# Turning the token rows of a GNN/attention/MoE layer: the attention branch added by TensorE in PSUM instead of by VectorE and GpSimd

## What is computed

```python
xn = _layernorm(x, axis=-1)
x = x + _L0_gnn_ref(xn, edge_index, edge_attr, ...) + _L0_mix_ref(xn[None], ...)[0]
x = x + _L0_ffn_ref(_layernorm(x, axis=-1)[None], ...)[0]

# end of _L0_gnn_ref
h = relu(h @ W1 + b1) @ W2 + b2
h = (h - h.mean(0)) * rsqrt(h.var(0) + eps) * gamma + beta
return relu(h)                          # y, the MLP's result
# end of _L0_mix_ref
return einsum('bnc,oc->bno', attn, Wproj) + bproj      # the attention rows
# start of _L0_ffn_ref: logits = xt @ Wr + br, top 2 of 8 experts for each node
```

## Time and profile before

| | us |
|---|---|
| time, median of 3 runs | 1186.91 (1179.77 to 1190.77) |
| span of the profiled execution | 1050.8 |
| median less span | 136.1 |
| TensorE matmuls busy | 964.7 (92%) |
| VectorE busy | 671.7 (64%) |
| GpSimd busy | 555.1 (53%) |
| ScalarE busy | 513.5 (49%) |

### The profile page before, as it was taken

How to read it: one execution, slowest core, us unless ns; L and a number is a source line. 1 busy time by engine, 2 the same in 40 slices (tenths; PEclk the granted TensorE clock), 3 DMA queues, 4 the chain that set the end, 5 groups by cost and what they waited for, 6 DMA issues and landing times.

```text
span 1050.8 us, 17977 instructions
## 1 busy us (share of the span) xinstructions
PE 964.7 (92%) x5112; PEld 810.3 (77%) x5113; DVE 671.7 (64%) x1274; ACT 513.5 (49%) x1036; POOL 555.1 (53%) x627
## 2 busy tenths in 40 slices
PE   5898999999999999999998961799999999999994
PEld 4677888888888888877775860778888888888884
DVE  5455565656655565578886778666666666666663
ACT  3644555555454545455554566444444444444442
POOL 3277777777777777777760040224253353444442
PEclk8899999999999999999998986899999999999998
DMA  9667788788888878998762028412545636635321
GB/s 246 197 154 237 255 267 253 250 268 266 260 254 262 269 247 267 278 313 270 239 202 86 26 89 316 181 26 40 204 90 174 220 50 213 192 73 160 98 38 21
DMA packets 85472, 198.30 MB, mean 189 GB/s; under 512 B 19785, under 2 KB 37139, under 8 KB 84378
## 3 DMA queue, kind: packets, MB, share of 16 engines
q1 hardware_dynamic: 55926, 131.60, 36.1%
q0 software_dynamic: 28752, 64.45, 25.5%
q10 hardware_dynamic: 724, 1.42, 0.5%
HBM read 147.86 MB, written 49.97 MB: 188 GB/s over the span
## 4 chain that ended last, share of the span: by engine, by line
POOL 29%; PE 29%; DMA 19%; issue 13%; DVE 7%; ACT 2%; POOLq 1%; SPq 0%; DVEq 0%; ACTq 0%
POOL work L758 29%; DMA out<-work,rowc 11%; PE banks L1141 6%; PE banks L1166 4%; DMA work<-token_table,tokc 4%; PE banks L470 3%; PE banks L446 3%; PE banks L1168 2%; PE banks L969 2%; PE banks L1054 2%; PE banks L1151 2%; DMA work<-in_edge_attr 1%; PE banks L1042 1%; DMA wts<-in_src 1%; DVE st L1776 1%
## 5 line engine op out<-in xcount | busy, mean ns | idle before, releaser
L758 POOL DMA_INDIRECT work<-node_table,srcT x391 | 379.5, 971 | 157.0 <-issue 117.6
L470 PE MATMUL banks<-work 128*128 128x256 f32 x780 | 179.1, 379 | 1.1 <-issue 1.1
L446 PE MATMUL banks<-w_edge,eaT 128*128 128x256 f32 x780 | 179.3, 380 | 0.0
L470 PEld LDWEIGHTS banks<-work 128*128 128x128 f32 x780 | 148.0, 190 | 21.8 <-issue 1.8
L446 PEld LDWEIGHTS banks<-w_edge,eaT 128*128 128x128 f32 x780 | 143.4, 191 | 16.8
L1166 PE MATMUL banks<-wsplit,hidT_hi 128*128 x416 | 153.3, 408 | 2.1 <-DVE hidT_lo L1908 2.1
L529 DVE TENSOR_TENSOR work<-banks,work 128x512 f32<-128x512 f32 x195 | 126.8, 682 | 26.1 <-DMA work<-node_table,srcT 15.2
L1141 PE MATMUL banks<-wsplit,xeT_hi 128*128 x416 | 134.3, 404 | 2.8 <-DVE xeT_lo L1915 2.8
L483 ACT COPY wts<-banks 128x256 f32<-128x256 f32 x66 | 24.6, 372 | 228.8 <-PE banks L470 227.8
L811 POOL DMA_INDIRECT out<-work,rowc x52 | 83.4, 1605 | 82.2 <-ACT work L1441 45.6
L1168 PE MATMUL banks<-wsplit,hidT_lo 128*128 x416 | 116.8, 281 | 0.0
(11 more groups left out here) (263 smaller groups left out, 1555.2 us busy)
## 6 DMA issues: line engine op xcount, KB each, us to landing
wsplit<-split_table SPq DMA_DIRECT2D x8, 4096.0 KB, 15.3
work<-in_edge_attr SPq DMA_DIRECT2D x65, 384.0 KB, 4.6
wts<-in_L_ffn_W SPq DMA_DIRECT2D x64, 256.0 KB, 4.9
split_table<-raw_hi SPq DMA_DIRECT2D x64, 256.0 KB, 3.0
split_table<-raw_lo SPq DMA_DIRECT2D x64, 256.0 KB, 4.3
work<-node_table,srcT POOLq DMA_INDIRECT x391, 4.2
xs<-in_x SPq DMA_DIRECT2D x8, 560.0 KB
wts<-in_L_ffn_b SPq DMA_DIRECT2D x8, 512.0 KB, 4.0
```

The lines of the kernel that those rows point to most:

```text
L446: last = nc.tensor.matmul(b[:, k * DIM:(k + 1) * DIM], eaT[:, u, 2 * q + k], w_edge[:], start=True, stop=True)
L470: last = nc.tensor.matmul(bank[5][:, 0:DIM], onehot[:, u, j], msg[:, u, j], start=(j == 0), stop=(j == GT - 1))
L758: pool.indirect_dma_start(out=xg[n % NB][0:rows, j], out_offset=None, in_=node_table, in_offset=bass.IndirectOffsetOnAxis(ap=srcT[0:rows, ...
```

## The change

The additions on VectorE and GpSimd are gone. TensorE multiplies the attention columns (`qT`) and then the relu's columns (`y_cur`) by the same `turn_route` into the same PSUM region: `attn_turn(q)` starts the sum and `y_turn(q)` ends it. ScalarE's relu now reads and writes in node order, and the step of five moves to the stationary operand of `y_turn`. `attn_turn` of the turns 2, 0, 1 and 3 stands ahead of the relu; the others stand one turn ahead of their `y_turn`, each behind the wait for its banks. SP's wait ahead of the first weight load is now for the last turn on TensorE.

```diff
@@ sync
-            sp.wait_ge(y_first, 1)
-            sp.wait_ge(y_sum, CHUNKS - 1)
+            sp.wait_ge(y_T, 3 * CHUNKS)
             load_weights(sp, 0)
@@ gpsimd
-            for c in range(1, CHUNKS):
-                pool.wait_ge(y_relu, 2 * c + 2)
-                nc.gpsimd.tensor_tensor(y_cur[c], y_cur[c], qT[:, :, c * CHUNK_TILES * TILE:(c + 1) * CHUNK_TILES * TILE],
-                                        ALU.add).then_inc(y_sum, 1)
@@ tensor
-            def y_turn(q):
-                c, b = q // 3, q % 3
-                if q == 0:
-                    pe.wait_ge(y_first, 1)
-                elif b == 0:
-                    pe.wait_ge(y_sum, c)
+            def turn(q, rows, first):
+                for m in range(2 if q % 3 < 2 else 1):
+                    k = 2 * (q % 3) + m
+                    for h in range(HALVES):
+                        last = nc.tensor.matmul(bank[2 * (q % 4) + m][0:TILE, h * P:h * P + P + EXPERTS], rows(h, k),
+                                                turn_route[:, h * (P + EXPERTS):(h + 1) * (P + EXPERTS)],
+                                                start=(first and h == 0), stop=(not first and h == 1), skip_group_check=True)
+                return last
+
+            def attn_turn(q):
+                if q == 1:
+                    pe.wait_ge(z2_ready, 2 * COL_CHUNKS)
                 if q == 3:
                     pe.wait_ge(xw_scaled, 2)
                 if q >= 4:
                     pe.wait_ge(lg_added, q - 3)
-                for m in range(2 if b < 2 else 1):
...
-                last.then_inc(y_T, 1)
-
+                lo = q // 3 * CHUNK_TILES
+                turn(q, lambda h, k: qT[:, h, (lo + k) * TILE:(lo + k + 1) * TILE], True)
+
+            def y_turn(q):
+                c = q // 3
+                pe.wait_ge(y_relu, 2 * c + 2)
+                turn(q, lambda h, k: y_cur[c][:, h, k:CHUNK_TILES * TILE:CHUNK_TILES], False).then_inc(y_T, 1)
+
+            pe.wait_ge(ao_ready, 2 * COL_CHUNKS)
+            for q in (2, 0, 1, 3):
+                attn_turn(q)
             for q in range(3 * CHUNKS):
+                if q >= 4:
+                    attn_turn(q)
                 y_turn(q)
@@ scalar
-                    nc.scalar.activation(y_cur[c][:, o].rearrange("q (k p) -> q k p", k=CHUNK_TILES), by_fives(hT, c)[:, o],
+                    nc.scalar.activation(y_cur[c][:, o], hT[:, o, c * CHUNK_TILES * TILE:(c + 1) * CHUNK_TILES * TILE],
                                          ACT.Relu, bias=bns[:, 3, o:o + 1], scale=bns[:, 2, o:o + 1]).then_inc(y_relu, 1)
@@ vector
-            dve.wait_ge(y_relu, 2)
-            nc.vector.tensor_tensor(y_cur[0], y_cur[0], qT[:, :, 0:CHUNK_TILES * TILE], ALU.add).then_inc(y_first, 1)
```

More of the change, by code:

```diff
@@ L344, in build @@
         y_relu = sem("y_relu")
-        y_sum = sem("y_sum")
-        y_first = sem("y_first")
         y_T = sem("y_T")
```

## The result

| | kernel before | changed kernel |
|---|---|---|
| time, median of 12 runs each | 1181.95 us (1166.25 to 1190.77) | 1187.62 us (1178.53 to 1198.39) |
| changed / before | | 1.0077, 95% interval 1.0041 to 1.0114 |
| span of the profiled execution | 1050.8 us | 1188.1 us |
| that execution's own time | not given | 1189.84 us |
| first relu's start to the end of the last statistics ("the stage") | 25.27 us | 34.93 us |

A forecast was written before the change was run, and what follows sets the result against it. VectorE's 3.45 us a chunk was taken as the node stage's bound, passing to TensorE after the change. Net +0.4 us for the passes and +1.1 for the clock, on 1186.91, gave 1188.4 us; range 1182 to 1195.5.

The forecast's parts named there:

- The sign that the prediction itself had set for being wrong: TensorE's turns: passes of over 0.15 us at full clock would show the forecast wrong, in favour of the open stepped load.
- What bounds the kernel: Node stage: VectorE at 3.45 us a chunk sets the pace only while TensorE delivers a chunk in less.
- the first rival: Node stage: TensorE's added passes are hidden and VectorE's pace stays the bound; -4.6 us, 1182.3; 8 in 100.
- Part 1: ScalarE's relu in node order: 0.90 us instead of 1.52, first pair done at 611.8 instead of 613.03.
- Part 2: Additions leave VectorE and GpSimd: VectorE's 1.47 us goes from the chain; removing GpSimd's four gains zero.
- Part 3: TensorE's first turns: `qT` turns 2, 0, 1 cost nothing; first `y_cur` turn at 612.1 to 612.2, 2.45 us earlier.
- Part 4: TensorE's turns become the bound: 100 `y_cur` passes at 0.129 and 72 `qT` at 0.115, sum 21.2 us; net +0.4 us.
- the third rival: TensorE's stepped load lies open, 100 x 0.07 us: 1193.2 at full clock, up to 1195 at half; 15 in 100.
- Part 5: TensorE's granted clock before the first turns: a fall lasts 4.4 us and loses 2.1; taken at half, +1.1 us.
- Part 6: First weight load issued later, at 633.6, delaying stores of chunks 3 and 4; ScalarE waits 0.6 us; cost 0, up to 1.
- After the stage: List building and experts: nothing changes, so the shift at the stage's end, +1.5 us, is the shift of the end.
- The rules that were weighed: Relu and TensorE's load: 16-byte-line rule spoke against the step, without a price; load-time rule gave 104 ns, hidden, time 1187.0.

The follow-up runs named there:

- experiment 6: Changed kernel with the old relu layout and contiguous loads, plus idle matmuls keeping TensorE's clock at full: stage 25.94 us.
- Experiment 5: Changed kernel with contiguous loads, the relu reading in node order and writing in steps: stage 26.37 us, relu 1488 ns.
- Experiments 3 and 8: Changed kernel, only chunk 0 summed on TensorE, contiguous loads, GpSimd adding the rest: stage 25.69 us; the second also with write-side step and idle matmuls: 25.16 us.
- experiment 4: Separate kernel of TensorE work alone, series differing in step, rows, moving columns or transposes: 0.116 us a pass at step 1, 0.217 at step 5.
- experiment 1: Changed kernel with the relu and stationary operand laid out as before, so all 200 passes load adjacent columns: stage 28.20 us.
- (2): Kernel before with only the stationary operand read in steps of five, relu and additions unchanged: stage 28.81 us.
- experiment 7: Changed kernel with ten idle matmuls ahead of the fourth attention turn to keep the clock at full: stage 34.41 us.
- experiment 10: Kernel before, unedited, profiled again: span 1194.2 us, stage 25.22 us; timed against itself, ratio 0.9984.
- experiment 9: Changed kernel, only chunks 0 and 1 summed on TensorE, contiguous loads, write-side step, idle matmuls: stage 22.39 us, timed ratio to before 0.9995.

## Why the prediction was right in the time and wrong by 8 us in the stage, step by step

- **The number.** The forecast of 1188.4 us and the measured 1187.62 lie 0.8 us apart, and that is luck. The sum started from 1186.91, the median of three runs, which twelve runs put at 1181.95, 5.0 us lower; the rise of 1.5 us was too small by about as much (5.7 between the medians, 9.1 by the ratio), and the two errors cancel. The sign that the prediction itself had set for being wrong, passes of over 0.15 us at full clock, came.
- **What bounds the kernel, and the first rival.** Right (what it calls chunks 2 and 3 are chunks 1 and 2 in the numbering of the kernel). TensorE's chunk became the bound and VectorE waits 15.3 us for it; experiment 6 shows that 40 contiguous passes alone (4.63 us) do that.
- **Part 1, the relu.** Right: 0.896 us on average for 0.90, the pair done 1.71 us after the start for 1.7. Experiment 5 shows that it is the step, on either side of ScalarE, that costs.
- **Part 2, the additions.** Right for what it claimed. Experiments 3 and 8 add that GpSimd's addition for chunk 1 is covered only as long as chunk 0 is late.
- **Part 3, the first turns.** Right but for the clock: the `qT` turns 2, 0 and 1 cost nothing, and the first `y_cur` turn starts 2.56 us after the relu for 2.0 to 2.1. Turn 3 started as forecast (738.95, 1.04 us after the relu); its eight passes took 1.52 us in place of 0.9, most of them at the half clock.
- **Part 4, the sum. This is the step that failed**, in one term: "If it paces the passes as in L877: 0.129 ... I take 0.129". A stepped pass takes 0.216. 100 x (0.216 - 0.129) = 8.7 us; with the 0.4 us of Part 4 that is +9.1, and with the 0.5 of the clock +9.6, where 9.66 were measured. The term lay outside its own bounds too (0.188 at most). The value taken and the upper bound both came from L877, whose loads belong to transposes; experiment 4 shows that row to be right for a transpose (0.136 with step six, 0.116 with step five) and of no use for an fp32 matmul, where the same steps cost 0.219 and 0.217. The upper bound used the 0.07 us by which a stepped load is longer in a transpose; in these matmuls it is 0.122 (310 against 188 ns), and 0.100 of it lie open. The count of passes, 200, was right. So the third rival, the stepped load that lies open, is what happened, at a higher price than it was given. It is shown three times: take the step out and 6.7 us go (experiment 1), put it alone into before and 3.5 come (2), measure it by itself (4). Between experiments 6 and 7, both at full clock, it is worth 8.5 us: 10.0 for 100 passes, less the 0.9 us by which the relu makes the first turn earlier and 0.3 us that TensorE stands idle in experiment 6; some 0.3 us are left over.
- **Part 5, the clock.** The sum took half of a possible 2.1 us. The clock did fall, for 3.4 us instead of 4.4, and it cost 0.5 us (experiment 7). Of the 15 passes that it hits 11 are stepped, and those take 0.22 to 0.23 at either level. With contiguous loads the price is 2.3 us (experiment 6 against 1).
- **Part 6, the late weight load.** Right in the mechanism: the load is issued at 770.71, ScalarE's store lands 15.5 us later (786.20) for 15 and holds it 1.03 us for 0.6, and the time from the last statistics to `tok_i` is 72.94 - 34.93 = 38.01 us against 37.93 before. The chain gives "DMA out<-xs" 14.61 us, yet it costs 0.1. It leaves no slack, as experiment 5 shows, where the same wait costs 0.8.
- **After the stage.** Right: +9.66 us at the stage's end, +9.74 at `tok_i`, +9.5 at the end (the last within the scatter of single profiles).
- **The time.** The prediction took the 136 us between span and median as lying outside the span. That is not where they lie: the changed kernel's execution is 1.7 us longer than its span (1189.84 against 1188.1), and experiment 10 puts before at 1194.2. This did no harm to a difference, but the sign that the profiled execution was not like the timed ones was there to be read.
- **The rules that were weighed.** "SBUF — State Buffer", section "Door 1: The DMA port swizzle", of the Trainium skill spoke against the change, and experiment 4 bears it out in kind: step 2 is free, and 8-byte steps put two columns into each 16-byte line, the two hits that the page asks for. The page also puts the free range at four fp32. Here the measurement differs: step 3 makes a pass half as long again (0.170) and step 4 costs as much as the wider ones (0.229), so for this load the free range ends below that. "TensorE: Matmul & The Clock Gate", section "LDWEIGHTS (loading the stationary operand)", gave 104 ns for 125 columns by columns over 1.2; for the contiguous load nothing here speaks against it (each record lasts 188 ns, but one load follows another every 116). For the stepped one it fails: 310 ns, one every 216.

What stays open: why a transpose pays so little for the stepped load and an fp32 pass so much (no run varied the type of an ordinary matmul); how much of experiment 9's gain the clock alone would give; and whether its 3 us at the list reach the timed median, which more runs than were made would have to show.

## What to carry to other kernels

Price an operand's layout on the instruction form that will read it: a row of nearly the same step in a transpose said 0.13 us, and the matmul took 0.22. In these matmuls a step of two elements was free, and one of three was not. Moving work onto TensorE "for free" by accumulating in PSUM is a question of periods: count the recorded passes (two for each fp32 matmul), multiply, and compare with the period of the engine that now sets the pace, here 4.6 against 3.45 us before any step is counted. The one version with a clearly shorter stage (22.39 us for 25.27) moved only two chunks of five, with contiguous loads and the clock kept up; whether the moved chunks or the clock made most of it was not separated, and the timed runs don't show it. And look at more than the time: a forecast within 0.1% of it stood on a price that was wrong by 8.7 us.

## What the runs showed of the hardware that had not been expected

- With a step in the free direction of its stationary operand an fp32 pass of 136 moving columns takes 0.170 us at step 3 and 0.217 to 0.240 from 4 to 9, against 0.116 at 1 and 2 (experiment 4). With 512 moving columns it takes 0.429, the stepped load hidden. With a step of five on the moving operand instead it takes (222.60 - 206.83) / 64 = 0.246.
- That price hardly depends on the granted clock: 66 rows with step five, in a stretch granted 0.66 on average, took 0.224, and with step six at 0.50 (164.04 - 149.53) / 64 = 0.227, where a contiguous pass goes from 0.116 to 0.23. That clock fell 4.6 us into the first series of 66 rows, with TensorE busy without a gap, and was back at full 3.1 us into the next series of 128. Windows of e4_loads on PE (us, PE busy (x), PEclk, DMA share, GB/s):

```profile
135.20:149.50 14.30, 14.30 (x65) 0.66 0.01 1
149.70:164.00 14.30, 14.30 (x65) 0.50 0.00 0
```

- The profile's chain can name a transfer for 14.61 us of which the kernel feels 0.1: beside the waited transfer another path of almost the same length ends. In experiment 5 it names it for 14.96, and 0.8 are felt.
- ScalarE pays for a step of five as much when it writes it (1.49 us for 625 columns) as when it reads it (1.52).
